# Second cross attention: where TensorE projects v, q and k within a step

## What is computed

```python
def _L1_xattn_ref(q, k, v, mask, w_q, w_k, w_v, w_o):   # q: layernorm(x); k, v: the context, 77 rows
    query, key_, value = proj(q, w_q), proj(k, w_k), proj(v, w_v)   # 16 heads of 8
    scores = jnp.einsum('bhqd,bhkd->bhqk', query, key_) / jnp.sqrt(D_K)
    scores = jnp.where(mask == 0, NEG, scores)
    attn = jax.nn.softmax(scores, axis=-1)
    out = jnp.einsum('bhqk,bhkd->bhqd', attn, value)
    return out.transpose(0, 2, 1, 3).reshape(B, -1, H * D_K) @ w_o.T
x = x + _L1_xattn_ref(_layernorm(x), ctx_1024, ctx_1024, mask, ...)
```

## Time and profile before

| | |
|---|---|
| runs | 1678.43, 1685.0, 1685.45 us; median 1685.0 us |
| profiled execution | 1682.17 us, its span 1680.3 us |
| mean granted TensorE clock | 0.967 of full speed |
| busy, share of the span | PE 88%, PEld 73%, DVE 75%, ACT 67%, POOL 53% |
| chain that ended last | PE 63%, DVE 17%, issue 7%, ACT 7%, POOL 3% |
| lines of this stage in the chain | L1310 3%, L1361 2%, L1386 2% |

### The profile page before, as it was taken

The page is one execution under the profiler, slowest core; times in us unless marked ns, Lnnn a source line. Parts: engine busy times, 40 slices in busy tenths (PEclk is TensorE's granted clock), DMA queues, the critical chain, the costliest instruction groups (busy, mean ns, idle before and its releaser), DMA issues.

```text
span 1680.3 us, 38581 instructions
## 1 busy us (share of the span) xinstructions
PE 1481.5 (88%) x12380; PEld 1233.8 (73%) x12443; DVE 1252.9 (75%) x3064; ACT 1119.4 (67%) x2631; POOL 894.1 (53%) x789
## 2 busy tenths in 40 slices
PE   4898888888877989898886899999889899999888
PEld 3777777677766876676765688888767688888766
DVE  6888888888856557777774788888655677777656
ACT  4887777677744547766674577787633687778632
POOL 4667777677631114444430777777500777777500
PEclk9999999999999999989997899999999899999999
DMA  9700000000012221100000000000000000000000
GB/s 384 296 1 10 11 10 10 7 17 12 12 59 67 85 84 43 33 13 16 16 14 4 10 16 16 15 14 15 10 12 3 6 15 15 16 15 14 10 18 38
DMA packets 75554, 61.30 MB, mean 36 GB/s; under 512 B 40256, under 2 KB 61120, under 8 KB 74688
## 3 DMA queue, kind: packets, MB, share of 16 engines
q1 hardware_dynamic: 71360, 51.69, 9.5%
q0 software_dynamic: 4096, 8.40, 1.7%
HBM read 21.30 MB, written 30.41 MB: 31 GB/s over the span
## 4 chain that ended last, share of the span: by engine, by line
PE 63%; DVE 17%; issue 7%; ACT 7%; POOL 3%; DMA 1%; SPq 0%; DVEq 0%; POOLq 0%; ACTq 0%
PE slot L459 6%; PE slot L1631 6%; PE slot L461 5%; PE slot L460 5%; PE slot L1614 4%; PE slot L1575 4%; PE slot L1584 3%; PE slot L1310 3%; PE slot L1649 3%; PE slot L516 3%; PE slot L1865 3%; PE slot L1361 2%; ACT c_pT L1386 2%; PE slot L1625 2%; PE slot L1176 2%
## 5 line engine op out<-in xcount | busy, mean ns | idle before, releaser
L1032 POOL TENSOR_TENSOR rs<-mv,nhalf 128x1 f32 (+1 forms) x160 | 98.6, 616 | 292.3 <-DVE mv L1027 222.7
L1781 POOL TENSOR_TENSOR d_A<-d_A,d_B 128x1024 f32<-128x1024 f32 x64 | 150.7, 2354 | 133.5 <-DVE d_B L1727 133.4
L1785 POOL TENSOR_TENSOR d_r<-d_vv,nhalf 128x16 f32<-128x16 f32 x64 | 186.5, 2914 | 47.8 <-DVE d_vv L1749 47.5
L731 ACT ACTIVATE d_p<-slot,d_nm,d_r 128x128 f32<-128x128 f32 x512 | 185.9, 469 | 25.8 <-DVE d_nm L1740 25.8
L731 ACT ACTIVATE a_p<-slot,a_nm,a_rq 128x77 f32<-128x77 f32 x512 | 164.0, 429 | 36.1 <-DVE a_nm L755 36.1
L1631 PE MATMUL slot<-d_v,d_pT 128*128 128x65 f32 x1024 | 121.8, 272 | 1.4 <-ACT d_pT L1668 1.4
L731 ACT ACTIVATE c_p<-slot,c_nm 128x77 f32<-128x77 f32 x512 | 117.5, 361 | 7.3 <-DVE c_nm L1416 7.2
L1631 PEld LDWEIGHTS slot<-d_v,d_pT 128*128 128x128 f32 x1024 | 119.4, 192 | 2.1 <-ACT d_pT L1668 1.8
L1708 DVE TENSOR_TENSOR d_A<-slot,T 128x1024 f32<-128x1024 f32 x64 | 78.3, 1224 | 49.8 <-PE slot L1575 49.6
L1386 ACT ACTIVATE c_pT<-slot 77x1024 f32<-77x1024 f32 x64 | 65.7, 1027 | 73.5 <-PE slot L1310 73.4
L1736 DVE TENSOR_REDUCE slot<-slot 128x8 f32<-128x1024 f32 x64 | 78.9, 1232 | 31.3 <-PE slot L1614 28.5
(11 more groups left out here) (285 smaller groups left out, 4607.2 us busy)
## 6 DMA issues: line engine op xcount, KB each, us to landing
routed<-zero SPq DMA_DIRECT2D x2, 9216.0 KB, 48.9
b_x<-routed SPq DMA_DIRECT2D x80, 64.0 KB
answers<-b_y SPq DMA_DIRECT2D x40, 128.0 KB
X<-in_x SPq DMA_DIRECT2D x2, 1024.0 KB, 7.4
d_zx<-Z SPq DMA_DIRECT2D x64, 32.0 KB
H<-Z SPq DMA_DIRECT2D x64, 32.0 KB
out<-f_o SPq DMA_DIRECT2D x8, 256.0 KB, 2.0
d_zx<-Z SPq DMA_DIRECT2D x64, 31.8 KB
```

Of the source, the lines that this page charges most:

```text
L731: i = e.activation(t["p"][:, h, :], R[slot][:, k // nbank, nk * (k % nbank):nk * (k % nbank) + nk], ACT.Exp, bias=t["nm"][:, h:h + 1], sca ...
L1032: return e.tensor_tensor(rs[:, bass.ds(b, 1)], mv[:, bass.ds(b, 1), 1:2].rearrange("p a b -> p (a b)"), nhalf[:, 0:1], ALU.pow)
L1781: e.tensor_tensor(t["A"][:, p, :], t["A"][:, p, :], t["B"][:, p, :], ALU.add).then_inc(S("d_key"), 1)
L1785: e.tensor_tensor(t["r"][:, it.m(2, 4), :], t["vv"][:, p, :], nhalf[:, 0:16], ALU.pow).then_inc(S("d_key"), 1)
```

## The change

v and q (two of the three projections of lag 3) move into the loop over the halves: they are issued at the end of the first half, behind its scores and ahead of the second half's transposes of P, together with the waits for c_sp, ac_xh (xT) and ac_ch (the context's copy). k stays behind the second half's scores. The count of c_proj, which follows k, stays where it was.

```diff
--- before.py
+++ after.py
@@ -1330,15 +1330,17 @@
                                               t["kb"][x][o:o + 32, it.m(4, 2), :, :].rearrange("p a b -> p (a b)"),
                                               start=False, stop=(n == 2))
                         mm.then_inc(S(("ac_Sa", "ac_Sb")[half]), 1)
+                    b = it.b(3)
+                    if half == 0 and b is not None:
+                        if it.seen(4):
+                            e.wait_ge(S("c_sp"), nth(it.upto(4), 3, 3))
+                        e.wait_ge(S("ac_xh"), count(b, base=NB))
+                        e.wait_ge(S("ac_ch"), count(b, base=NB))
+                        e.matmul(R[0][0:SK, 0, 256:384], t["c"][:, it.m(3, 4), :], l1[:, 2, :], start=True, stop=True)
+                        e.matmul(R[0][:, 0, 0:128], l1[:, 0, :], t["xT"][:, it.m(3, 2), :], start=True, stop=True)
                 b = it.b(3)
                 if b is not None:
-                    if it.seen(4):
-                        e.wait_ge(S("c_sp"), nth(it.upto(4), 3, 3))
-                    e.wait_ge(S("ac_xh"), count(b, base=NB))
-                    e.wait_ge(S("ac_ch"), count(b, base=NB))
                     c = t["c"][:, it.m(3, 4), :]
-                    e.matmul(R[0][0:SK, 0, 256:384], c, l1[:, 2, :], start=True, stop=True)
-                    e.matmul(R[0][:, 0, 0:128], l1[:, 0, :], t["xT"][:, it.m(3, 2), :], start=True, stop=True)
                     e.matmul(R[0][:, 0, 128:128 + SK], l1[:, 1, :], c, start=True, stop=True).then_inc(S("c_proj"), 1)
                 if it.b(5) is not None or it.b(2) is not None or it.b(6) is not None:
                     if it.seen(6):
```

## The result

The change is slower. Its median is 1694.54 us (1686.88 to 1705.32, 15 runs), that of before 1681.05 us (1677.71 to 1691.96, 15 runs); the ratio is 1.0066, 95% interval 1.0048 to 1.0083. The forecast was 1681.0 us, the range 1673 to 1688. The profiled execution of the change took 1705.3 us, the longest of its runs, so what follows leans on medians where it can. Of the 23.2 us between the two profiled spans, 6.3 had come up before the stage's first transpose of xn (623.7 us before, 630.0 now), where the change does nothing.

The account below looks back on a forecast made before the run. GpSimd's gather was taken to set the regular step (4.76 + 3.47 + 0.28 = 8.51 us). 1682.2 - 2.1 - 0.5 = 1679.6, raised 1.4 towards the runs' median, gave 1681.0 us, range 1673 to 1688.

Parts of the forecast that it names:

- v and q into the gap: Gap ahead of the second transposes: hides 0.30 of v and q's 0.39 us, leaving 0.09 on the second half.
- k alone: Ahead of the products with P only k remains, taking 0.38 us, so products could begin at 763.88.
- products 0.30 earlier: Products with P in a regular step begin 0.30 us earlier, at 763.88, 4.64 after the step's first load instead of 4.94.
- The wait that comes along: q's wait for xT, now ahead of the second transposes: costed at nothing in a regular step, bounds 0 and 1.1 us.
- Rival two: The wait for xT holds the second half, deciding from about 1.0 us late; 9.8 us lost, 1692.0; chance 0.06.
- The step is set by the gather: Regular step: gather 4.76 after first load, xn 3.47 later, next load 0.28 later; period 8.51 us, whenever products begin.
- a matter of instructions reaching TensorE: Holes in the products: instructions don't reach TensorE until a fixed time after the gather begins, last hole ending 2.80 to 2.87 later.
- The sum, 2.6 us gained: Whole kernel: 2.1 us from seven steps plus 0.5 from the other 23, taking 1682.2 to 1679.6.
- term of 2.1 us from the seven steps without a gather: Five steps without a gather in the products and two with a late one gain 0.30 us each: 2.1.
- rise of PE's issue wait to 23 us: TensorE's "issue" wait ahead of the products (L1361) would grow from 16.4 us by about 0.3 per step to some 23.
- Rival three: TensorE's clock: one half-clock stretch more or less, 6.8 us in either direction, 1674 or 1688; chance 0.08, all "same".
- The base of the forecast: Sum taken off the profiled execution's 1682.2, then set 1.4 up, halfway towards the shown runs' median of 1685.0.

Follow-up runs that it names:

- kernel 2: The change, but v and k in the gap and q with its wait for xT behind the second scores: 1691.32 us, 1.0037 against the kernel before.
- kernel 10: The change again, unaltered, on the chip of a later comparison: 1692.31 us, 1.0047 against the kernel before.
- kernel 16: The change without the stage's gathers (zeros instead), repeated on a chip where the kernel before takes 1678.54: 1654.03 us, 0.9841 against the kernel before.
- kernel 8: The change without the stage's gathers (zeros instead), on the chip where the kernel before takes 1643.5: 1651.09 us, 1.0051 against the kernel before.
- kernel 13: The kernel before with GpSimd's gathers held until TensorE's products are done, repeated where before takes 1678.54: 1655.96 us, 0.9881 against the kernel before.
- kernel 15: The kernel before without the stage's gathers (zeros instead), repeated where before takes 1678.54: 1648.37 us, 0.9831 against the kernel before.
- kernel 1: The change with v and q computed a second time at their old place ahead of k: 1686.88 us, 1.0029 against the kernel before.
- kernel 3: The kernel before with GpSimd's gathers moved earlier, behind the copy of c_c: 1689.78 us, 1.0041 against the kernel before.
- kernel 4: The change with GpSimd's gathers moved earlier, behind the copy of c_c: 1684.28 us, 1.0011 against the kernel before.
- kernel 9: The kernel before, unchanged, run again for its own profile: 1684.28 us, 1.0007 against the reference runs of before.
- kernel 11: The change with only v in the gap, q (with its wait for xT) and k behind the second scores: 1684.9 us, 0.9994 against the kernel before.
- kernel 12: The change with k moved into the gap too, so v, q and k all there: 1696.43 us, 1.0082 against the kernel before.
- kernel 5: The kernel before with gathers held until TensorE's products are done, on the chip where before takes 1643.5: 1651.87 us, 1.0057 against the kernel before.
- kernel 6: The change with gathers held until TensorE's products are done, on the chip where before takes 1643.5: 1737.13 us, 1.0568 against the kernel before.
- kernel 7: The kernel before without the stage's gathers (zeros instead), on the chip where before takes 1643.5: 1643.98 us, 1.0003 against the kernel before.
- kernel 14: The change with gathers held until TensorE's products are done, repeated where before takes 1678.54: 1740.22 us, 1.037 against the kernel before.
- kernel 17: The change with gathers held until TensorE's products are done and GpSimd's c_c copy ahead of that hold: 1664.21 us, 0.9899 against the kernel before.

## Why the prediction was wrong, step by step

- **v and q into the gap, 0.30 hidden, 0.09 left over; k alone; products 0.30 earlier.** Right to 0.04: 2.35, 4.68 and no idle time in the step shown.
- **The wait that comes along, at nothing.** Right in the regular part (about 1.3 us in all, and kernel 2 loses without it). Wrong in the steps without a gather: held for xT, they take 7.68 in place of 7.11 in kernel 10, and 0.24 to 0.28 more a step in kernels 16 and 8. Rival two had this wait, but let it decide only from 1 us on.
- **The step is set by the gather.** Right, to 0.01 us in the step shown. Over the whole stage it holds as well: in the kernel before, 21 of the 22 steps with holes have the last one end 2.79 to 2.87 us behind the first gather's start. Kernels 13 and 15 confirm that the gathers, where they meet the products, hold the stage: 20 and 30 us. That the holes are a matter of instructions reaching TensorE is still only inferred. Kernel 15 is also what the rule of the Trainium skill (Runtime: NRT & Kernel Launch, "Instruction fetch mechanics") leads one to expect, fetching hidden in straight code; if the holes are a matter of fetching, those of 0.59 and 0.64 in the step above speak against it where gathers run.
- **The sum, 2.6 us gained.** Not seen. At equal half-clock time kernel 10 stands at 1684.9 against 1684.1, and the change's first 15 runs at 1685.3 against the 1684.0 of the kernel before beside kernels 1 to 4 (its own 15 runs have no clocks on record): about 1 us slower. With slopes from 0.25 to 0.43 the first pair reads 2.9 slower to 1.0 faster. So a small gain is neither shown nor excluded. Its term of 2.1 us from the seven steps without a gather is the weak one: it took 0.30 from each, and of those looked at one gained 0.25 and the next lost 0.57. The forecast rise of PE's issue wait to 23 us did not come either. A step at half clock works longer through the instructions it has, so less of the same hole is idle time; this is a reading, not tested.
- **Rival three is the step that failed.** The text had the mechanism: the filled gap changes what TensorE does ahead of a low stretch. Its sum has no term for that. It priced it as one stretch more or less, 6.8 us, took both signs as equally likely, gave it 0.08 and called all of that "same". Measured: in the profiled executions the stretches within the stage are 10 in place of 4 (7 in place of 5 in the repeats, kernels 10 and 9), and in the medians half-clock time rose by some 20 to 30 us. On the chip of kernel 10 it went from 121 to 144, 23 x 0.35 = 8.0 us, where the medians are 7.1 apart. In the first comparison the clocks of the kernel before are not on record but for its profiled execution, with 111 us; from there to the change's 142 is 31 x 0.35 = 11 us of the 13.5 between the medians. The price per us comes from the scatter among runs of one kernel, so these are estimates. In this kernel it went up both times; with the gathers early the new order had the lower half-clock time (kernels 3 and 4), so "in either direction" was right in general, and the even odds were wrong here.
- **The base of the forecast.** It took the sum off the profiled execution, 1682.2, and added 1.4 towards the 1685.0 of three runs. That the 1681.0 equals the median of before over 15 runs, 1681.05, is chance; from that base the sum would have given 1678.5, 16 us under the result.
- **What the price should have rested on.** The earlier trace rows showed a stretch at half clock with TensorE busy throughout, and the text went on to the gaps. The order of the change shows that v and q leave the place directly ahead of the products, the ones that run dry. Kernels 1, 2, 11, 10 and 12 point to just that: 113 against 114 with the work put back, 135 against 114 with v and k gone, and 126, 144 and 146 against 121 as one, two and three leave.

Open: what in the sequence of busy and idle makes the clock fall. Runs show when it falls more often (holes there, less work ahead of them), not why. Kernel 1 put the work back by doing it twice; a kernel with other work of the same length in that place, or the same amount elsewhere, would tell place from amount. The split between the holes' position and the work moved was not tried by itself either; it would need the same order with holes of another size.

## What to carry to other kernels

If an engine runs dry for 0.6 us where it waits for nothing of its own, look at what another engine starts some us before, and try to shift that first. Filling an idle gap of TensorE with work taken from beside another gap is not neutral when its clock is at stake; compare the mean granted clock of all runs, and the time at equal half-clock time, before reading a change of half a per cent as a matter of schedule. Before a queue is made to wait for an engine, list what is queued behind the wait and whether that engine needs it.

## What was not expected of the hardware

- With GpSimd's indirect DMAs come holes of 0.6 us in TensorE's stream of small matmuls, the last ending 2.79 to 2.87 us behind the first gather's start, and about 30 us in the whole kernel (kernel 15); but only while the products run, not over the scores (kernels 3 and 13).
- Chips differ. The kernel before has medians of 1678.5 to 1685.2 us on three and 1643.5 on one, and on that one leaving the gathers out gains nothing (1.0003). The 35 us between are near what kernel 15 gains elsewhere. And the four kernels that have no such holes take almost the same on both chips, 5 to 8 against 13 to 16: 1651.9 and 1656.0, 1737.1 and 1740.2, 1644.0 and 1648.4, 1651.1 and 1654.0. So the chips differ mainly where gathers meet the products. That the holes are missing on that chip suggests itself; no profile of the kernel before was taken there, so it stays open.
- Half-clock time differs from run to run of one kernel on one chip, and goes with most of that spread: slope 0.35, correlation 0.96 over the change's 15 runs; 0.25 to 0.43 and 0.88 to 0.98 over 31, 31 and 24 of the kernel before.
- A wait of 2.3 us a step on average, 3.7 at most, went with a rise of half-clock time from 116 to 209 us (kernels 17 and 14). The kernel lost 76 us, more than the wait's own 59.
